# Preactivation convolution chain: the sums over the batch of layers 1 and 3 made by GpSimd instead of VectorE

## The chip, the cores and the metric

The kernel runs on 1 core of one Trainium2 chip. The metric is device time in microseconds (us), the median of several executions of the whole kernel. Times in the trace are us from the start of the span of one profiled execution.

## The reference, cut to what matters

```python
x = x + L0(gn(x))          # x is [32, 32, 32, 32], float32
x = x + L1(gn(x))
x = x + L2(gn(x))
x = x + L3(gn(x))

def L0(x, weight, bias_p, gamma, beta):         # L2 is the same with its own arrays
    wb = sign(weight) * mean(abs(weight))       # one 3x3 kernel for each place of the image
    out = einsum('bchwk,ochwk->bohw', patches(x), wb) + bias_p
    mean, var = out.mean((0, 2, 3)), out.var((0, 2, 3))      # one of each a channel
    out = relu(gamma * (out - mean) * rsqrt(var + 1e-5) + beta)
    return sign(out) * mean(abs(out))
```

L1 is a convolution with weights of its own for each place, without signs or statistics; L3 multiplies x, its squares and all products of pairs in a row by weights. `gn` is a normalisation over 16 groups of channels. In the kernel the layers are numbered 0 to 3; the change is in layers 0 and 2. The mean of `out` needs the sum of the convolution's result over the batch (32 samples) for each channel and place: 128 partitions x 256 places, kept in `row_sums`. The sum of its product with the bias, a part of the variance, is made from the same array.

## The kernel before

The image lies in SBUF as 128 partitions x 8 blocks (`BLOCKS`, index m) x 1024 elements, with the batch innermost. A convolution layer runs over 32 chunks (n = 4m + j); each has a weight load of 1152 KB, a stretch of matmuls called a piece here, and a stage on each of the other engines. The engines' programs are written out in order by hand, each with semaphores to the others. In layers 0 and 2, for chunk n:

- SyncE loads the weights into one of 8 slots of `wring`, once both VectorE and ScalarE are done with chunk n - 8.
- GpSimd (loop over n at the end of `xn_of`, `low_half`, `copy_near`): two operations of `xn_of` (L267) normalise piece e = n + 6 into a ring of 4; `low_half` (L372) waits for ScalarE's `high_half` and writes the low float16 half of piece n + 5; `copy_near` (L383) waits until piece n - 4 has been multiplied and copies the neighbours. The normalisation ends with e = 31, at n = 25; from n = 26 on only `copy_near` is left. The first 8 pieces are normalised by VectorE (`FRONT`).
- ScalarE: `high_half` (L517) of piece n + 6, which waits for `xn_of` of that piece; `load_beyond` (L526), two DMAs of 32 KB that bring rows of the neighbouring blocks, for which the pieces up to n + 4 must be normalised and piece n - 4 multiplied; `sign_of` (L509 and L510) on the weights; for n % 4 in (1, 2) and n > 4, `square_half` (L537) on a half of an earlier block's result.
- TensorE: piece n, once `near` and `beyond` of n are there and the signs of n are made. The two PSUM banks of a block must be free before its pieces 0 and 1.
- VectorE: the sum of the absolute weights of chunk n (L747), and after chunks 4m + 3 and 4m + 4 `evacuate(e)` for e = 2m and 2m + 1: it waits until the bank's pieces are done, transposes the bank from PSUM into `scratch` (L739), and reduces the 32 batch elements of each of 16 places into `row_sums` (L741).

After the last piece the chain goes over `evacuate(15)`, the sum of the absolute sums (L757), the bias product (L760) and some twenty small operations to the batch statistics of the layer, and from there to the next layer.

`sum_squares` on GpSimd (L393, L397) is not changed, but is built like the added code: in layers 0 and 1, before the convolution, it adds halves of 1024 elements in five steps with a wait for GpSimd's own semaphore after each of the first four:

```python
while width > B:
    pool.tensor_tensor(sq[:, 0:width], sq[:, 0:width], sq[:, width:2 * width], ALU.add).then_inc(halved, 1)
    halvings[0] += 1
    pool.wait_ge(halved, halvings[0])
    width //= 2
```

Of the kernel before, what the change touches and what calls it, by code (L numbers as in the profile page):

```python
# [9 lines left out]
ALU = mybir.AluOpType  # L10
ACT = mybir.ActivationFunctionType
X = mybir.AxisListType.X

P = 128
B = C = H = W = 32
# [5 lines left out]
BLOCKS = 8  # L21
PIECES = 4
# [52 lines left out]
def build(nc, x, w_conv, bias, gamma_beta, w_pairs, mats, sel_rows, sel_index, out):  # L75
    ctx = ExitStack()
    with ctx:
        def sb(name, shape, dt):
            return ctx.enter_context(nc.sbuf_tensor(name, shape, dt))

        def sem(name):
            return ctx.enter_context(nc.semaphore(name))

        def sems(name, n):
            return [sem(f"{name}{i}") for i in range(n)]
# [13 lines left out]
        stats = sb("stats", [P, 6, 512], F32)  # L99
# [6 lines left out]
        row_sums = sb("row_sums", [P, BLOCKS * W], F32)  # L106
# [43 lines left out]
        bank_free = sems("bank_free", 2)  # L150
# [20 lines left out]
        abs_red = sems("abs_red", 2)  # L171
        abs_total = sems("abs_total", 2)
        rows_summed = sem("rows_summed")
        rows_squared = sem("rows_squared")
        bn_sums_in = sems("bn_sums_in", 2)
        bn_sums = sems("bn_sums", 2)
# [34 lines left out]
        states = [(state_a, state_b), (state_a, state_b), (state_b, state_a)]  # L211

        def blk(t, m):
            return t[:, m * BLOCK:(m + 1) * BLOCK]

        def rows_of(t, e):
            return t[:, e * 512:(e + 1) * 512]

        def normed(layer, m, j):
            aux = states[layer][1]  # L220
            first = (m + 1) * BLOCK + j * PIECE
            return aux[:, first:first + PIECE]
# [5 lines left out]
        def order(m, j):  # L228
            return 2 * j + m if m < 2 else PIECES * m + j

        def needed(n):

            m, j = divmod(n, PIECES)
            return order(min(m + 1, BLOCKS - 1), j)
# [13 lines left out]
        def wait_normed(eng, layer, e):  # L248
            if layer == 1 and e < FRONT:
                eng.wait_ge(front_made, FRONT + e + 1)  # L250
            else:
                eng.wait_ge(norm_made[layer], e + 1 - (FRONT if layer == 1 else 0))
# [99 lines left out]
        def _(pool):  # L352
# [6 lines left out]
            def xn_of(layer, e, made):  # L359

                if layer != 1:
                    pool.wait_ge(norm_made[layer], e - XSLOTS + 1)
                sub, mul = normalise(pool, layer, e)
                sub().then_inc(centred, 1)
                centre[0] += 1
                pool.wait_ge(centred, centre[0])
                mul().then_inc(made, 1)

            def low_half(layer, e):
                pool.wait_ge(hi_made, CHUNKS * (layer // 2) + e + 1)  # L370
                hv = halves(layer, e)
                pool.tensor_tensor(hv[:, 1, :], xn_ring[:, e % XSLOTS, :], hv[:, 0, :], ALU.subtract).then_inc(norm_made[layer], 1)  # L372

            def copy_near(layer, n):

                m, j = divmod(n, PIECES)
                wait_normed(pool, layer, order(m, j))
                if n >= PIECES:
                    pool.wait_ge(conv_done, CHUNKS * layer + n - PIECES + 1)
                dst, src = near[:, j, :], normed(layer, m, j)  # L380
                if layer != 1:
                    dst, src = dst.bitcast(F16), src.bitcast(F16)
                pool.tensor_copy(dst, src).then_inc(near_made, 1)  # L383
# [3 lines left out]
            def sum_squares(layer, m):  # L387

                pool.wait_ge(squares[layer], m + 1)
                sq = blk(states[layer][1], m)  # L390
                width = BLOCK // 2
# [4 lines that stand above are left out]
                    width //= 2  # L396
                pool.tensor_tensor(red[:, 1, m * B:(m + 1) * B], sq[:, 0:B], sq[:, B:2 * B], ALU.add).then_inc(gn_red_pool[layer], 1)  # L397

            for layer in range(3):
                if layer < 2:  # L400
                    for m in range(DVE_SQUARES, BLOCKS):
                        sum_squares(layer, m)
                pool.wait_ge(gn_ready[layer], 1)
                ready = 0
                for n in range(CHUNKS):
                    upto = min(CHUNKS, needed(n) + 3)
                    for e in range(ready, upto):
                        if e >= FRONT:
                            xn_of(layer, e, norm_made[1] if layer == 1 else xn_made)
                        if layer != 1 and e:  # L410
                            low_half(layer, e - 1)
                        if layer != 1 and e == CHUNKS - 1:
                            low_half(layer, e)
                    ready = max(ready, upto)
                    copy_near(layer, n)

            def copy_ring(k):

                if k % (2 * GROUP) == 0 and k < NK:
                    pool.wait_ge(parts_in[k // GROUP // 2] if k else half_in, 16 * 2 * G)  # L420
                if k == GROUP:
                    pool.wait_ge(parts_in[0], 16 * 2 * G)
                if k >= GROUP:
                    pool.wait_ge(gathered, (k - GROUP + 1) * PT)
                for side in range(2):
                    if side:
                        pool.wait_ge(ring_made, 2 * k + 1)
                    pool.tensor_copy(ring[side * 2 * W:(side + 1) * 2 * W, k % GROUP, :].rearrange("p (g n) -> p g n", g=G),  # L428
                                     parts[0:2 * W, k // KPART % 2, :, k % KPART * C4 * B:(k % KPART + 1) * C4 * B]
                                     ).then_inc(ring_made, 1)  # L430
                pool.wait_ge(ring_made, 2 * k + 2)
# [213 lines left out]
        def _(dve):  # L645
# [26 lines left out]
            def sum_rows(side, src, m, layer):  # L672
                dve.tensor_reduce(red[:, side, m * B:(m + 1) * B], blk(src, m).rearrange("p (h b) -> p b h", b=B), X,
                                  ALU.add).then_inc(gn_red[layer], 1)

            for layer in range(3):
# [10 lines left out]
                width = MB if layer < 2 else 512  # L687
# [16 lines left out]
                if layer == 1:  # L704
# [4 lines left out]
                    for e in range(2 * BLOCKS):  # L709
                        m, h = divmod(e, 2)  # L710
# [17 lines left out]
                m2 = layer // 2  # L728
# [5 lines left out]
                def evacuate(e):  # L734

                    m, h = divmod(e, 2)
                    raw = rows_of(scratch, e).rearrange("p (w b) -> p w b", b=B)
                    dve.wait_ge(conv_done, CHUNKS * layer + PIECES * m + 3 + h)
                    dve.transpose(raw, psum[:, h, :].rearrange("p (w o) -> p w o", o=C)).then_inc(bank_free[h], 1)  # L739
                    dve.wait_ge(bank_free[h], 1 + BLOCKS * layer + m + 1)  # L740
                    dve.tensor_reduce(row_sums[:, e * 16:(e + 1) * 16], raw, X, ALU.add).then_inc(rows_summed, 1)  # L741

                for n in range(CHUNKS):
                    dve.wait_ge(w_in[slot(layer, n)], 16 * loads(layer, n))
                    if n == 0 and m2:
                        dve.wait_ge(abs_red[0], 1)
                    dve.tensor_reduce(abs_sums[:, n:n + 1], wring[:, slot(layer, n), 0:ABS_DVE],  # L747
                                      X, ALU.add, apply_absolute_value=True).then_inc(abs_made, 1)
                    if n % PIECES == 3:
                        evacuate(2 * (n // PIECES))  # L750
                    if n % PIECES == 0 and n:
                        evacuate(2 * (n // PIECES) - 1)
                evacuate(2 * BLOCKS - 1)

                dve.wait_ge(abs_made, CHUNKS * (m2 + 1))
# [357 lines left out]
```

## Time and profile before

| | us |
|---|---|
| median of 3 runs | 734.14 (733.12 to 734.63) |
| the profiled execution's own time | 732.94 |
| its span, first to last instruction | 731.1 |
| VectorE busy | 566.7 (78%) |
| TensorE busy | 497.6 (68%) |
| ScalarE busy | 431.5 (59%) |
| GpSimd busy | 420.1 (57%) |

The busy times are sums over a program with stages of different kinds, so the shares of the whole say little of one stage. The convolution of layer 0 takes the span from about 40 to 141 us, that of layer 2 from about 328 to 427 us; the rows below are taken inside these two. Engines are PE (TensorE), DVE (VectorE), ACT (ScalarE), POOL (GpSimd) and SP (SyncE); ACTq is ScalarE's sequencer, which issues its DMAs. L383 is line 383 of the kernel.

### The profile page before, as it was taken

What the parts mean: (1) busy time and instruction counts of PE and PEld (TensorE: products, weight loads), DVE (VectorE), ACT (ScalarE), POOL (GpSimd) and SP (SyncE); (2) the same over time, 40 slices, a digit from 0 to 9 for tenths busy, and PEclk for the clock granted to TensorE, in tenths of its full rate; (3) what the DMA queues carried; (4) which work ended last, traced back from release to release, by engine and by line L of the source; (5) the groups of instructions that cost most, each with busy time, mean ns of one, the idle gap of its engine ahead of it and who ended that gap; (6) DMA issues with size and microseconds to landing.
All of it is one profiled execution on the core that took longest, in us unless ns stands there. A gap on an engine that the chain in (4) does not pass through costs nothing.

```text
span 731.1 us, 53320 instructions
## 1 busy us (share of the span) xinstructions
PE 497.6 (68%) x24392; PEld 388.3 (53%) x24392; DVE 566.7 (78%) x709; ACT 431.5 (59%) x717; POOL 420.1 (57%) x653
## 2 busy tenths in 40 slices
PE   3546656609479999806666623626898888887898
PEld 4535655509368888605656521204565555554565
DVE  4799999898833635389999989955688788887787
ACT  5359999574011212317999938324567766666665
POOL 3388885004445651029888200537779878878672
PEclk9858889758799999955888975966899999999999
DMA  8949999500179999946999930015789999999996
GB/s 329 422 146 397 400 399 397 231 0 1 32 275 376 379 390 392 412 192 230 395 395 398 368 138 0 1 26 163 270 302 402 368 353 406 364 340 384 333 387 246
DMA packets 38882, 209.09 MB, mean 286 GB/s; under 512 B 7216, under 2 KB 14384, under 8 KB 18352
## 3 DMA queue, kind: packets, MB, share of 16 engines
q1 hardware_dynamic: 29376, 201.67, 72.2%
q10 hardware_dynamic: 9216, 6.30, 2.8%
q0 software_dynamic: 240, 0.53, 0.2%
q8 instruction: 22, 0.36, 0.2%
q14 instruction: 28, 0.23, 0.1%
HBM read 193.79 MB, written 4.19 MB: 271 GB/s over the span
## 4 chain that ended last, share of the span: by engine, by line
PE 37%; DVE 19%; DMA 13%; issue 11%; ACT 9%; POOL 8%; ACTq 2%; SPq 0%; DVEq 0%; POOLq 0%
PE psum L902 15%; PE psum L1015 7%; DMA wring<-in_pairs 6%; PE psum L989 5%; PE psum L926 5%; ACT signs L510 4%; DMA beyond<-state_b 4%; POOL xn_ring L267 3%; ACT state_b L640 2%; DVE state_b L862 2%; DVE state_a L807 2%; PE psum L1001 2%; DMA beyond<-state_a 2%; POOL state_a L372 2%; ACTq L526 2%
## 5 line engine op out<-in xcount | busy, mean ns | idle before, releaser
L862 DVE TENSOR_TENSOR state_b<-psum,state_b 128x512 f32<-128x512 f32 x256 | 167.6, 686 | 52.2 <-ACT state_b L640 48.2
L902 PE MATMUL psum<-signs,near 64*32 64x96 f16 (+3 forms) x6528 | 128.8, 221 | 98.1 <-DMA beyond<-nothing 37.8
L640 ACT ACTIVATE state_b<-psum 128x512 f32<-128x512 f32 x256 | 142.0, 595 | 81.3 <-PE psum L989 77.0
L902 PEld LDWEIGHTS psum<-signs,near 64*32 64x32 f16 (+1 forms) x6528 | 116.1, 105 | 106.8 <-issue 106.3
L747 DVE TENSOR_REDUCE abs_sums<-wring 128x1 f32<-128x2048 f32 x64 | 142.8, 2276 | 0.1
L510 ACT ACTIVATE signs<-wring 128x2304 f16<-128x2304 f32 x64 | 134.9, 2108 | 0.0
L1015 PE MATMUL psum<-state_b,wring 128*32 128x32 f32 x8192 | 104.5, 201 | 11.0 <-issue 5.3
L1015 PEld LDWEIGHTS psum<-state_b,wring 128*32 128x32 f32 x8192 | 86.9, 112 | 40.6 <-issue 21.6
L902 PE MATMUL psum<-wring,near 64*32 64x96 f32 (+5 forms) x3264 | 96.2, 242 | 14.8 <-DMA beyond<-nothing 10.5
L989 PE MATMUL psum<-signs,sel 64*128 64x512 f16 x516 | 88.1, 395 | 26.2 <-POOL signs L428 13.9
L428 POOL COPY signs<-wring 64x512 f16<-64x512 f16 x130 | 85.7, 659 | 30.7 <-PE psum L989 24.3
L902 PEld LDWEIGHTS psum<-wring,near 64*32 64x32 f32 (+1 forms) x3264 | 87.7, 109 | 21.8 <-issue 19.8
L383 POOL COPY near<-state_b 128x512 f16<-128x512 f16 (+1 forms) x64 | 34.4, 539 | 66.7 <-PE psum L902 33.8
L902 PE MATMUL psum<-signs,beyond 32*32 32x96 f16 (+2 forms) x2176 | 65.6, 218 | 0.0
L902 PEld LDWEIGHTS psum<-signs,beyond 32*32 32x32 f16 x2176 | 56.4, 103 | 4.8
L447 POOL COPY wring<-state_b 32x256 f32<-32x256 f32 x128 | 50.6, 395 | 10.1
L713 DVE STREAM_TRANSPOSE state_b<-psum 128x512 f32<-128x512 f32 x16 | 11.5, 717 | 57.6 <-PE psum L912 57.0
L989 PEld LDWEIGHTS psum<-signs,sel 64*128 64x128 f16 x516 | 23.8, 93 | 47.5 <-ACT state_b L640 25.5
L902 PE MATMUL psum<-wring,beyond 32*32 32x96 f32 (+2 forms) x1088 | 48.8, 239 | 0.0
L571 ACT ACTIVATE signs<-state_a 128x1024 f32<-128x1024 f32 x8 | 8.5, 1058 | 67.3 <-PE psum L912 60.5
L393 POOL TENSOR_TENSOR state_b<-state_b 128x512 f32<-128x512 f32 (+3 forms) x24 | 16.7, 698 | 54.0 <-ACT state_b L501 52.6
L372 POOL TENSOR_TENSOR state_a<-xn_ring,state_a 128x256 f16<-128x256 f32 x32 | 22.3, 698 | 41.2 <-ACT state_a L517 41.1
(153 smaller groups left out, 881.6 us busy)
## 6 DMA issues: line engine op xcount, KB each, us to landing
wring<-in_w SPq DMA_DIRECT2D x96, 1152.0 KB, 10.2
wring<-in_pairs SPq DMA_DIRECT2D x64, 1152.0 KB, 9.0
state_a<-in_x SPq DMA_DIRECT2D x8, 512.0 KB, 9.9
beyond<-state_b ACTq DMA_DIRECT2D x112, 32.0 KB, 5.9
wring<-signs SPq DMA_DIRECT2D x56, 64.0 KB, 4.9
out<-state_a SPq DMA_DIRECT2D x7, 512.0 KB, 10.8
beyond<-state_a ACTq DMA_DIRECT2D x56, 32.0 KB, 6.1
beyond<-nothing ACTq DMA_DIRECT2D x24, 32.0 KB, 4.7
```

The costliest lines, as they stand in the source:

```text
L372: pool.tensor_tensor(hv[:, 1, :], xn_ring[:, e % XSLOTS, :], hv[:, 0, :], ALU.subtract).then_inc(norm_made[layer], 1)
L383: pool.tensor_copy(dst, src).then_inc(near_made, 1)
L428: pool.tensor_copy(ring[side * 2 * W:(side + 1) * 2 * W, k % GROUP, :].rearrange("p (g n) -> p g n", g=G), parts[0:2 * W, k // KPART % 2, ...
L447: pool.tensor_copy(own_x[beside * W:(beside + 1) * W, g % 2, cols], x_sq[g * W:(g + 1) * W, half, :]).then_inc(own_copied, 1)
L510: act.activation(signs[:, n % PIECES, :], wring[:, slot(layer, n), :], ACT.Sign).then_inc(signs_made, 1)
L640: act.activation(left[:, n % LSLOTS, :], psum[:, n % ASLOTS, :], ACT.Copy, scale=1.0 / HALF_SCALE / HALF_SCALE).then_inc(left_made, 1)
L747: dve.tensor_reduce(abs_sums[:, n:n + 1], wring[:, slot(layer, n), 0:ABS_DVE], X, ALU.add, apply_absolute_value=True).then_inc(abs_made, 1)
L862: dve.tensor_tensor(feats[:, n % FSLOTS, :], psum[:, ASLOTS + n % BSLOTS, :], left[:, n % LSLOTS, :], ALU.mult).then_inc(feats_made, 1)
L902: last = pe.matmul(psum[g * B:(g + 1) * B, bank, (a * C) % 512:(a * C) % 512 + (b - a) * C], acts[q, j, s, k, :], weights[q, j, kind, s, ( ...
L926: pe.matmul(psum[:, 4, first * B:end * B], same_half, by_h[:, h, first:end, :], start=(first == 0 and h == 0), stop=(h == H - 1), skip_gro ...
L989: last = pe.matmul(psum[:, bank, :], sel[half, t % PT * P:(t % PT + 1) * P], ring[half, t // PT, :], start=True, stop=True)
L1015: last = pe.matmul(psum[g * W:(g + 1) * W, 6 + s // HALF, col:col + B], wt[:, t % PT, c, g, :], f[:, g, c, :], start=False, stop=(t % (HAL ...
```

## The change

In layers 0 and 2 `evacuate` on VectorE keeps only the transpose. GpSimd gets `sum_rows(layer, e)`: it waits for the transpose of half block e, adds the upper half of the batch to the lower in five steps (16 places x 16, 8, 4, 2, 1 results a partition), with a wait for its own semaphore after every step, and writes the same 16 columns of `row_sums`. Sixteen calls a layer: after `copy_near` of n = 5, 7, 9, ..., 31 (e = 0 to 13), and e = 14 and 15 behind the loop. VectorE waits for `rows_summed` before the bias product, as it did.

```diff
@@ -396,6 +397,27 @@
+            added = [0]
+
+            def sum_rows(layer, e):
+
+                m2 = layer // 2
+                pool.wait_ge(bank_free[e % 2], 1 + BLOCKS * layer + e // 2 + 1)
+                raw = rows_of(states[layer][1], e).rearrange("p (w b) -> p w b", b=B)
+                tree = stats[:, 1, :].rearrange("p (k w b) -> p k w b", k=2, b=B // 2)
+                width = B // 2
+                src = raw
+                while width > 1:
+                    dst = tree[:, width.bit_length() % 2, :, 0:width]
+                    pool.tensor_tensor(dst, src[:, :, 0:width], src[:, :, width:2 * width], ALU.add).then_inc(rows_added, 1)
+                    added[0] += 1
+                    pool.wait_ge(rows_added, added[0])
+                    src = dst
+                    width //= 2
+                pool.tensor_tensor(row_sums[:, e * 16:(e + 1) * 16].unsqueeze(2), src[:, :, 0:1], src[:, :, 1:2], ALU.add
+                                   ).then_inc(rows_summed, 1)
+                pool.wait_ge(rows_summed, 2 * BLOCKS * m2 + e + 1)
+
@@ -413,6 +435,10 @@
                             low_half(layer, e)
                     ready = max(ready, upto)
                     copy_near(layer, n)
+                    if layer != 1 and n > PIECES and n % PIECES in (1, 3):
+                        sum_rows(layer, 2 * (n // PIECES - 1) + n % PIECES // 2)
+                for e in range(2 * BLOCKS - 2, 2 * BLOCKS) if layer != 1 else ():
+                    sum_rows(layer, e)
@@ -737,8 +763,6 @@
                     dve.transpose(raw, psum[:, h, :].rearrange("p (w o) -> p w o", o=C)).then_inc(bank_free[h], 1)
-                    dve.wait_ge(bank_free[h], 1 + BLOCKS * layer + m + 1)
-                    dve.tensor_reduce(row_sums[:, e * 16:(e + 1) * 16], raw, X, ALU.add).then_inc(rows_summed, 1)
```

## Rows read from the trace of the kernel before

**Rows 1.** Busy time by window, two stretches of each changed layer.

```profile
core 0: us, PE busy (x) PEld busy (x) DVE busy (x) ACT busy (x) POOL busy (x), PEclk, DMA share, GB/s
55.53:113.04 57.51, 37.52 (x2604) 34.17 (x2608) 55.79 (x40) 57.51 (x97) 50.20 (x77) 0.83 1.02 398
342.10:399.17 57.07, 39.31 (x2581) 35.44 (x2585) 54.64 (x39) 56.80 (x97) 50.14 (x77) 0.80 1.02 395
113.04:140.74 27.70, 18.59 (x1354) 16.78 (x1336) 25.42 (x20) 25.03 (x37) 7.49 (x13) 0.88 0.94 366
399.17:427.39 28.22, 17.68 (x1360) 15.91 (x1360) 26.47 (x21) 25.03 (x37) 7.51 (x13) 0.94 0.96 370
```

**Rows 2.** Timeline: `copy_near` of n = 5 and 24, and ScalarE's signs of n = 24.

```profile
55.53 0.61 POOL L383 COPY near<-state_b 128x512 f16<-128x512 f16 x1
113.04 0.61 POOL L383 COPY near<-state_b 128x512 f16<-128x512 f16 x1
...
115.37 2.11 ACT L510 ACTIVATE signs<-wring 128x2304 f16<-128x2304 f32 x1
...
342.10 0.61 POOL L383 COPY near<-state_a 128x512 f16<-128x512 f16 x1
399.17 0.61 POOL L383 COPY near<-state_a 128x512 f16<-128x512 f16 x1
```

**Rows 3.** Waits of GpSimd, 55 to 113 us and then 342 to 399 us.

```profile
POOL state_b L372 <- ACT state_b L517: 5.8, 10, 0.6
...
POOL state_a L372 <- ACT state_a L517: 5.4, 9, 0.6
```

**Rows 4.** Groups of instructions, 60 to 100 us: busy, mean ns, idle before.

```profile
L747 DVE TENSOR_REDUCE abs_sums<-wring 128x1 f32<-128x2048 f32 x14 | 31.3, 2276 | 0.0
...
L267 POOL TENSOR_TENSOR xn_ring<-xn_ring,stats 128x256 f32<-128x256 f32 x14 | 10.2, 730 | 1.1
...
L372 POOL TENSOR_TENSOR state_b<-xn_ring,state_b 128x256 f16<-128x256 f32 x13 | 8.7, 672 | 4.0 <-ACT state_b L517 4.0
L383 POOL COPY near<-state_b 128x512 f16<-128x512 f16 x13 | 7.9, 611 | 0.0
...
L739 DVE STREAM_TRANSPOSE state_b<-psum 128x512 f32<-128x512 f32 x7 | 5.0, 707 | 1.4 <-PE psum L902 1.4
...
L741 DVE TENSOR_REDUCE row_sums<-state_b 128x16 f32<-128x512 f32 x7 | 4.8, 686 | 0.2
```

**Rows 5.** Groups of instructions on GpSimd, whole span: halvings of `sum_squares`.

```profile
L393 POOL TENSOR_TENSOR state_b<-state_b 128x512 f32<-128x512 f32 x6 | 7.7, 1281 | 52.6 <-ACT state_b L501 52.6
L393 POOL TENSOR_TENSOR state_b<-state_b 128x256 f32<-128x256 f32 x6 | 4.4, 733 | 0.5
L393 POOL TENSOR_TENSOR state_b<-state_b 128x128 f32<-128x128 f32 x6 | 2.7, 457 | 0.5
L393 POOL TENSOR_TENSOR state_b<-state_b 128x64 f32<-128x64 f32 x6 | 1.9, 321 | 0.5
L397 POOL TENSOR_TENSOR stats<-state_b 128x32 f32<-128x32 f32 x6 | 1.5, 253 | 0.5
```

**Rows 6.** Timeline of ScalarE's sequencer, the two issues of one `load_beyond`.

```profile
111.92 0.51 ACTq L526 DMA_DIRECT2D beyond<-state_b  x1
...
112.46 0.61 ACTq L526 DMA_DIRECT2D beyond<-state_b  x1
```

**Rows 7.** The chain that ended last, end of layer 0's convolution: start, length.

```profile
132.73 6.26 DMA beyond<-state_b
...
139.08 1.64 PE psum L902 x128
...
140.74 0.73 DVE state_b L739
...
142.09 0.21 DVE abs_sum L757
142.30 0.34 DVE stats L760
```

More of the change, by code:

```diff
@@ L173, in build @@
         rows_summed = sem("rows_summed")
+        rows_added = sem("rows_added")
         rows_squared = sem("rows_squared")
```

## Prediction

> **What bounds the kernel now.** I read the page first, then busy time by window, because the shares of the whole mix stages. Inside the two changed layers I cut two stretches: A, from GpSimd's copy_near of n = 5 to that of n = 24 (19 stages), and B, from there to the end of the convolution. [Rows 1] show that in A nothing is idle but TensorE: ScalarE is busy 57.51 us of 57.51 in layer 0 and 56.80 of 57.07 in layer 2, VectorE 55.79 and 54.64, GpSimd 50.20 and 50.14, the DMA share is 1.02. So the question is how much room GpSimd has, and whether relief of VectorE is worth anything.
>
> Next I read the waits of GpSimd alone. In A it waits 5.8 us in layer 0 and 5.4 us in layer 2, all of it in front of low_half for ScalarE's high_half [rows 3]. Without these waits its 19 stages take 57.51 - 5.8 = 51.7 us and 57.07 - 5.4 = 51.7 us, so 2.72 us a stage. That agrees with the groups: 2 x 0.730 + 0.672 + 0.611 = 2.74 us of operations [rows 4]. One block (4 stages) is 10.9 us of GpSimd against a pace of 57.51 / 19 x 4 = 12.1 us. **The room is 1.2 us a block, 0.6 us for each of the two added sums.** In B there is much: 7.5 us of work in 28 us [rows 1].
>
> GpSimd and ScalarE go in lockstep in A. ScalarE can't take high_half of a piece before GpSimd's xn_of of it, and everything behind high_half in ScalarE's program (load_beyond, the signs) waits with it. TensorE needs the beyond and the signs. So a late GpSimd stage is a late stage of everything.
>
> **The price of one sum.** The trace has no sum_rows, but the halvings of sum_squares are the same instruction at the sizes 256, 128, 64 and 32: 733, 457, 321, 253 ns [rows 5]. The size 16 isn't there; the last two steps differ by 68 ns for 32 elements, so 253 - 34 = 219 ns. Sum 1.98 us. Each wait for GpSimd's own semaphore leaves 0.5 / 6 = 0.08 us idle [rows 5], and sum_rows has five: 0.40 us. As instructions there overlap their neighbours' ends by some hundredths, I take **2.35 us**. Lower bound: 1.98 us, with no gap at all. Upper bound: the operands are 16 short rows with a stride, and no row shows such rows; if every element cost as two do, the steps cost as 512, 256, 128, 64 and 32: 1.281 + 0.733 + 0.457 + 0.321 + 0.253 = 3.05, with the gaps 3.45 us. I take the low side because the xn_of operations, with a mean broadcast over 8 rows, cost 730 ns [rows 4], as the plain 256 does.
>
> The Trainium skill (GPSIMD Engine Reference, section 7, Performance pitfalls) says that reads from SBUF whose inner step is above 8 bytes cost some 2.9 cycles an element in place of 1.9. No row of this trace shows such a read. Only the last step, with 16 results, has an inner step of 64 bytes; at the 1.2 GHz with which section 3.1 of that page reckons, an estimate by it is 16 more cycles, 0.01 us a sum. Were all 496 results of the five steps to pay it, the estimate would be 0.4 us a sum, which would make the change about 9 us dearer than I forecast.
>
> **Stretch A.** Ten sums fall in it (n = 5, 7, ..., 23). If GpSimd now sets the pace, its waits for ScalarE go, since ScalarE needs 12.1 us a block and GpSimd 10.9 + 2 x 2.35 = 15.6. The stretch takes 51.7 + 23.5 = 75.2 us. Layer 0: 75.2 - 57.5 = +17.7. Layer 2: 75.2 - 57.1 = +18.1. **Together +35.8 us.**
>
> Does the added wait for the transpose cost more? Behind it in GpSimd's queue is the next xn_of, for which all wait. For even e it needs piece n - 3 multiplied. That piece's beyond is issued about 1.6 us into its GpSimd stage, is there some 0.5 + 6.3 us after that, the matmuls take 1.6 us or somewhat more [rows 6, 7], the transpose 0.7 [rows 4]: about 11 us after the start of stage n - 3. Stage n gets to its sum at 3 x 2.72 + 2.35 + 2.72 = 13.2 us. VectorE sits free in front of the transpose by then. I take 0, with a margin of 2 us; at slower matmuls, 0.5 us for each even e would be 5 us in all.
>
> **What VectorE gains: 0.** It loses 16 reductions of 0.686 us a layer [rows 4], 11 us, and goes from 4 x 2.276 + 2 x (0.707 + 0.686) = 11.9 us a block to 10.5. Nothing takes it up in A, where it then waits for GpSimd's pace; in B ScalarE is the next limit. If the sums cost GpSimd nothing, ScalarE's 12.1 us a block would still cover it.
>
> **Stretch B.** GpSimd has per block 4 x 0.61 + 2 x 2.35 = 7.1 us of work in some 11 to 12 us, and its copy_near runs ahead of TensorE, so the sums are hidden there. ScalarE is the limit again at its old pace, but starts B less behind GpSimd: now its signs of n = 24 begin 115.37 - 113.04 = 2.33 us after GpSimd's copy [rows 2]. When it has waited for GpSimd, only the two issues of load_beyond, 0.51 + 0.61 us [rows 6], and 0.4 us for the absolute values lie between high_half and the signs, which comes to 1.0 us after the copy. **-1.3 us a layer, -2.6.** The last piece in layer 0 waits for a beyond that takes 6.26 us under a full DMA load until 139.0 [rows 7], where ScalarE's last signs end near 137.6. In the changed kernel the weights have been loaded ahead, and the beyond lands earlier, so up to this 1.4 us come back: **-1.3**. In layer 2 the next weights are being loaded at that time either way: 0.
>
> **The end of each convolution.** Now from the end of the transpose, 140.74 + 0.73 = 141.47, to the bias product at 142.30 it is 0.83 us, with the reduction and L757 in it [rows 7]. In the changed kernel GpSimd must finish e = 15: 2.35 us and two hand-overs of some hundredths, 2.40 us, with L757 beside it. e = 14 is done by then, as its transpose comes a piece earlier. 2.40 - 0.83 = 1.57 us a layer, **+3.1 us**.
>
> **Sum.** 35.8 - 2.6 - 1.3 + 3.1 = **+35.0 us**. The profiled execution took 732.94 us (span 731.1), so 767.9; the median of the runs is 1.2 us above it, so **769 us**.
>
> **Rivals.**
> - *The short rows are dear* (chance 0.09). Price 3.45 us: 20 x 1.1 = +22 in A and +2.2 at the ends, so +59 us, 793 us. For it: no row has operands of this form. Against it: the broadcast rows of xn_of cost nothing.
> - *More is given back in B* (0.08). ScalarE is busy only 25.03 us of 27.70 and 28.22 [rows 1]. If all of its idle there went, 2.7 + 3.2 us, in place of the 1.3 that I took for the last beyond, the result is 4.6 us lower, 764 us; with the price at its lower bound (20 x 0.37 + 0.7 = 8 us less), 756 us.
> - *GpSimd's load stays hidden* (0.03). If the lockstep had more play than I read, only the ends remain: +3 us, 737 us. Against it: the waits of [rows 3] are all the slack there is.
> - *VectorE is the bound, and its relief counts* (0.03). SyncE's loads wait for VectorE's sums of absolute weights as well as for the signs, and VectorE is busy 97% of A [rows 1]. If it sets the pace through the weight slots, 16 reductions a layer come off: 2 x 11.0 = -22, and +3 at the ends, 715 us. It decides where a sum costs GpSimd less than its 0.6 us of room. Five instructions at 0.18 us, what the halvings extrapolate to at no element at all (253 - 32 x 2.1), are already 0.9 us.
>
> **The numbers.** My forecast has a chance of 0.77. The range takes in the lower price with more given back (756) and most of the way to the dear price (793): 755 to 788, with something above for dear rows and something below for the two rivals near or under the old time. Faster by over 0.2% (about what a measurement of this kernel can tell) is the last rival, 0.03; within 0.2% is 0.01; slower is the rest, 0.96.
>
> **What the profile should show.** (1) Five steps of sum_rows near 733, 457, 321, 253 and 219 ns, a sum in 2.3 to 2.4 us. (2) In A GpSimd at about 98% of a stretch of 75 us with no waits for ScalarE; ScalarE and VectorE with gaps, the DMA share down to about 0.8. (3) The chain that ended last running through GpSimd's L267, L372, L383 and the new line in both layers. (4) Some 2.4 us between the last transpose and the bias product. (5) Layer 1 and layer 3 as they were. **What would make it wrong:** steps whose time doesn't follow the count of elements; waits for the transposes in front of the first step; a play between GpSimd and ScalarE that takes several us.

## The result and the profile after

The changed kernel takes 770.56 us (median of 4 runs, 765.71 to 776.52) against 733.75 us. The ratio of the executions is 1.0488, with a 95% interval of 1.0441 to 1.0535, so the kernel is slower by 32 to 39 us; the medians differ by 36.8 us. Ratios here leave out executions more than 1.5% above the fastest of their kernel, and are not exactly the quotients of the medians. Forecast were 769 us, between 755 and 788. The profiled execution took 772.41 us, with a span of 770.6.

The title counts the layers from 1; here, as in the kernel, the changed ones are layers 0 and 2. Stretch A runs from GpSimd's copy_near of n = 5 to that of n = 24, and stretch B from there to the start of the last transpose. First the groups of instructions on GpSimd over the whole span. These are the five steps of sum_rows, the first once from each of the two state tensors; the halvings to compare them with are in [rows 5]:

```profile
L412 POOL TENSOR_TENSOR stats<-stats 128x128 f32<-128x128 f32 x32 | 14.5, 452 | 2.5
...
L412 POOL TENSOR_TENSOR stats<-state_a 128x256 f32<-128x256 f32 x16 | 11.7, 730 | 8.3 <-DVE state_a L765 8.2
L412 POOL TENSOR_TENSOR stats<-state_b 128x256 f32<-128x256 f32 x16 | 11.7, 730 | 6.8 <-DVE state_b L765 6.7
L412 POOL TENSOR_TENSOR stats<-stats 128x64 f32<-128x64 f32 x32 | 10.2, 318 | 2.5
...
L412 POOL TENSOR_TENSOR stats<-stats 128x32 f32<-128x32 f32 x32 | 7.6, 239 | 2.5
L417 POOL TENSOR_TENSOR row_sums<-stats 128x16 f32<-128x16 f32 x32 | 6.9, 214 | 2.5
```

730 + 452 + 318 + 239 + 214 ns = 1.95 us. The first four are as the halvings of the same size or a little below, so the 16 short rows cost nothing that can be seen. The last step, whose operands lie 64 bytes apart, has no halving of its size: it is 5 ns below what the halvings give for 16 results (219), and 9 ns above what its own neighbour gives (239 - 16 x 2.1 = 205). The idle column shows 2.5 / 32 = 0.08 us before each step.

Now a piece of the chain that ended last, inside stretch A of layer 0 (start, length). The chain is nothing but GpSimd's own work:

```profile
101.56 0.55 POOL near L384
102.11 0.70 POOL stats L412
102.81 0.07 issue
...
104.12 0.23 POOL row_sums L417
104.34 0.07 issue
104.41 0.73 POOL xn_ring L268
```

The 0.07 us of issue behind each step is the wait for the engine's own semaphore. The next xn_of starts only after the fifth of them. The chain gives a sum 104.41 - 102.11 = 2.30 us, but it cuts instructions where they overlap. The timeline of the same place shows the copies that begin and end the stages:

```profile
98.83 0.61 POOL L384 COPY near<-state_b 128x512 f16<-128x512 f16 x1
...
101.50 0.61 POOL L384 COPY near<-state_b 128x512 f16<-128x512 f16 x1
...
106.52 0.61 POOL L384 COPY near<-state_b 128x512 f16<-128x512 f16 x1
```

A stage without a sum takes 101.50 - 98.83 = 2.67 us, one with a sum 5.02. **A sum lengthens its stage by 2.35 us.** Nine stages of the one kind and ten of the other make 9 x 2.67 + 10 x 5.02 = 74.2 us.

The same stretches as in [rows 1], A of both layers and then B of both layers:

```profile
core 0: us, PE busy (x) PEld busy (x) DVE busy (x) ACT busy (x) POOL busy (x), PEclk, DMA share, GB/s
55.15:129.60 74.45, 48.28 (x2781) 43.69 (x2771) 50.82 (x31) 61.05 (x98) 68.90 (x128) 0.71 0.95 355
358.04:432.28 74.24, 47.27 (x2728) 43.04 (x2732) 50.20 (x30) 61.20 (x98) 68.83 (x128) 0.71 0.94 358
129.60:155.21 25.61, 15.40 (x1171) 13.82 (x1156) 20.12 (x13) 23.12 (x35) 16.82 (x37) 0.87 0.68 253
432.28:459.70 27.42, 18.87 (x1216) 17.22 (x1216) 20.84 (x13) 23.23 (x35) 16.31 (x36) 0.74 0.63 235
```

Stretch A grew by 74.45 - 57.51 = 16.9 us and 74.24 - 57.07 = 17.2 us. ScalarE, at 100% before, is idle for 13 us of it now; VectorE, at 97%, for 24 us. GpSimd is busy for 68.9 us (93%), and the other 5.5 us are gaps between its instructions; no wait for another engine is listed in either stretch. Stretch B shrank by 27.70 - 25.61 = 2.1 us in layer 0 and by 28.22 - 27.42 = 0.8 us in layer 2.

The transfers fell less than the stretch grew: 355 GB/s x 74.45 us are 26.4 MB in A of layer 0, where it was 398 x 57.51 = 22.9 MB, and B has 6.5 MB in place of 10.1. So some three of the weight loads of 1152 KB moved from B into A.

Last the end of layer 0, on GpSimd and then on VectorE:

```profile
153.16 0.73 POOL L412 TENSOR_TENSOR stats<-state_b 128x256 f32<-128x256 f32 x1 [4.32 <-DVE state_b L765]
...
156.07 0.73 POOL L412 TENSOR_TENSOR stats<-state_b 128x256 f32<-128x256 f32 x1 [0.64 <-DVE state_b L765]
156.88 1.17 POOL L412 TENSOR_TENSOR stats<-stats 128x128 f32<-128x128 f32 x3
158.13 0.21 POOL L417 TENSOR_TENSOR row_sums<-stats 128x16 f32<-128x16 f32 x1
...
155.21 0.72 DVE L765 STREAM_TRANSPOSE state_b<-psum 128x512 f32<-128x512 f32 x1 [2.20 <-PE psum L926]
155.85 0.18 DVE L781 TENSOR_REDUCE abs_sum<-abs_sums 128x1 f32<-128x64 f32 x1
158.38 0.42 DVE L784 TENSOR_TENSOR stats<-row_sums,bias 128x256 f32<-128x256 f32 x1 [2.35 <-POOL row_sums L417]
```

VectorE has its transpose done at 155.93 and starts the bias product at 158.38, 2.45 us later. In the same view of the kernel before it is 142.22 - 141.46 = 0.76 us (0.83 in [rows 7], where the chain again cuts the overlap). From the start of the last transpose it is 3.17 us in place of 1.48.

Up to the bias product of layer 2, which starts at 462.95 us instead of 428.87, 34.1 of the 39.5 us between the two profiled spans have arisen. The other 5.4 us arose in layer 3, which isn't changed; the last experiments are on them.

### The profile page after: what moved, and what is told of

It reads as the page before. It is cut to its first block, busy times and chain, and to the rows that moved or that the text cites. A ratio compares the mean times of both kernels' runs of the same rounds, so it can differ in the third digit from the quotient of the medians.

```text
span 770.6 us, 53474 instructions
## 1 busy us (share of the span) xinstructions
PE 518.3 (67%) x24392; PEld 405.4 (53%) x24392; DVE 544.5 (71%) x677; ACT 436.5 (57%) x717; POOL 480.2 (62%) x813
## 4 chain that ended last, share of the span: by engine, by line
PE 34%; POOL 24%; DVE 17%; issue 8%; DMA 7%; ACT 6%; SPq 2%; ACTq 1%; POOLq 0%; DVEq 0%
PE psum L926 14%; POOL xn_ring L268 7%; PE psum L1039 5%; POOL stats L412 5%; PE psum L1013 5%; PE psum L950 4%; DMA wring<-in_pairs 4%; POOL near L384 3%; POOL signs L454 2%; ACT signs L536 2%; DVE xn_ring L268 2%; DVE state_a L831 2%; POOL state_a L373 2%; DMA beyond<-state_b 2%; PE psum L1025 2%
## 5 line engine op out<-in xcount | busy, mean ns | idle before, releaser
L926 PE MATMUL psum<-signs,near 64*32 64x96 f16 (+3 forms) x6528 | 145.1, 236 | 113.0 <-DMA beyond<-nothing 35.7
L926 PEld LDWEIGHTS psum<-signs,near 64*32 64x32 f16 (+1 forms) x6528 | 130.9, 114 | 122.4 <-issue 120.0
L926 PE MATMUL psum<-signs,beyond 32*32 32x96 f16 (+2 forms) x2176 | 73.5, 231 | 0.0
L384 POOL COPY near<-state_b 128x512 f16<-128x512 f16 (+1 forms) x64 | 34.1, 536 | 58.3 <-PE psum L926 26.8
L926 PEld LDWEIGHTS psum<-signs,beyond 32*32 32x32 f16 x2176 | 63.3, 111 | 5.7
L473 POOL COPY wring<-state_b 32x256 f32<-32x256 f32 x128 | 50.4, 394 | 10.1
L1013 PEld LDWEIGHTS psum<-signs,sel 64*128 64x128 f16 x516 | 23.8, 93 | 46.5 <-ACT state_b L666 24.7
L926 PEld LDWEIGHTS psum<-wring,beyond 32*32 32x32 f32 x1088 | 43.2, 106 | 3.5 <-issue 0.3
L950 PE MATMUL psum<-state_a,mats_sb 128*128 128x96 f32 (+1 forms) x256 | 33.9, 303 | 16.2 <-DMA state_a<-in_x 11.0
```

Of the source, the lines that this page charges most:

```text
L473: pool.tensor_copy(own_x[beside * W:(beside + 1) * W, g % 2, cols], x_sq[g * W:(g + 1) * W, half, :]).then_inc(own_copied, 1)
L926: last = pe.matmul(psum[g * B:(g + 1) * B, bank, (a * C) % 512:(a * C) % 512 + (b - a) * C], acts[q, j, s, k, :], weights[q, j, kind, s, ( ...
L950: pe.matmul(psum[:, 4, first * B:end * B], same_half, by_h[:, h, first:end, :], start=(first == 0 and h == 0), stop=(h == H - 1), skip_gro ...
L1013: last = pe.matmul(psum[:, bank, :], sel[half, t % PT * P:(t % PT + 1) * P], ring[half, t // PT, :], start=True, stop=True)
```

## The experiments

Each ratio is against the kernel before, run beside it on the same chip. The kernel before had medians of 732.5 to 736.8 us there, and single executions of 724.8 to 741.1, so it scatters more than its first runs had shown; the 95% intervals are given for that reason. In the diffs, three dots stand for what is left out.

**VectorE's relief alone** (no_sums). The sums over the batch are left out on VectorE, and GpSimd does nothing in their place; `row_sums` is set to zero at the start.

```diff
                     dve.transpose(raw, psum[:, h, :].rearrange("p (w o) -> p w o", o=C)).then_inc(bank_free[h], 1)
-                    dve.wait_ge(bank_free[h], 1 + BLOCKS * layer + m + 1)
-                    dve.tensor_reduce(row_sums[:, e * 16:(e + 1) * 16], raw, X, ALU.add).then_inc(rows_summed, 1)
...
-                dve.wait_ge(rows_summed, 2 * BLOCKS * (m2 + 1))
+                dve.wait_ge(bank_free[1], 1 + BLOCKS * (layer + 1))
```

> The kernel before without its reductions on VectorE and with nothing in their place: the sums over the batch in both layers are left out (row_sums stays at zero). My theory (VectorE's relief is worth nothing beside ScalarE at 100% and the weight DMA at its full share): only the 0.6 us behind the last transpose of each layer goes, 733.7 - 1.2 = 732.5 us, 731.5 to 733.5. Rival (VectorE sets the pace through the weight slots): 16 x 0.686 us a layer come off, 712 us.

Measured: 729.46 us against 732.51, ratio 0.9973 (0.9933 to 1.0013). That is 2 us less by the ratio and 3 by the medians, with an interval that includes no change. The median lies 2 us below the expected range, and the kernel before ran 1.2 us below the 733.7 on which that range was built. The windows of stretch A in both layers:

```profile
54.76:111.51 56.75, 35.36 (x2596) 32.22 (x2600) 50.11 (x30) 56.75 (x97) 50.12 (x78) 0.89 1.02 397
343.49:400.18 56.69, 35.59 (x2580) 32.30 (x2581) 49.09 (x30) 56.69 (x97) 50.06 (x77) 0.88 1.02 395
```

VectorE falls from 55.8 to 50.1 us of busy time in A of layer 0, and ScalarE stays at 100%. The rival of 712 us is refuted. The stretches are 0.8 and 0.4 us shorter than in the first profile of the kernel before, but that is no gain of the relief: with VectorE's reductions in place the same stretch took 57.51, 57.07, 56.70 and 58.13 us in the two profiles of the kernel before, and 56.70 to 56.72 us in the unchanged layers of the kernels layer0_only, layer2_only and delay48 below. What the relief does give is at the two ends, where the bias product starts 0.75 us after the last transpose in place of 1.48: 1.5 us in all.

**GpSimd's load alone** (both_sum). VectorE reduces as before; GpSimd does all of sum_rows as well.

```diff
                     dve.transpose(raw, psum[:, h, :].rearrange("p (w o) -> p w o", o=C)).then_inc(bank_free[h], 1)
+                    dve.wait_ge(bank_free[h], 1 + BLOCKS * layer + m + 1)
+                    dve.tensor_reduce(row_sums[:, e * 16:(e + 1) * 16], raw, X, ALU.add).then_inc(rows_summed, 1)
...
-                pool.tensor_tensor(row_sums[:, e * 16:(e + 1) * 16].unsqueeze(2), src[:, :, 0:1], src[:, :, 1:2], ALU.add
-                                   ).then_inc(rows_summed, 1)
-                pool.wait_ge(rows_summed, 2 * BLOCKS * m2 + e + 1)
+                pool.tensor_tensor(tree[:, 1, :, 0:1], src[:, :, 0:1], src[:, :, 1:2], ALU.add).then_inc(rows_added, 1)
+                added[0] += 1
+                pool.wait_ge(rows_added, added[0])
...
                 dve.wait_ge(rows_summed, 2 * BLOCKS * (m2 + 1))
+                dve.wait_ge(rows_added, 10 * BLOCKS * (m2 + 1))
```

> VectorE reduces as in the kernel before, and GpSimd does the whole of sum_rows as well, with its last step into a spare column. My theory (all of the loss is GpSimd's load): the stretch of 19 stages at 74.4 us as in the changed kernel, the end of each layer as there, so 765 to 772 us, as the changed kernel. Rival (the loss has a part that comes from VectorE's changed timing, such as late transposes): below 760 us. Rival (VectorE's relief has given something back in the changed kernel): above 774 us.

Measured: 769.55 us, ratio 1.0511 (1.0420 to 1.0602). Stretch A takes 74.97 and 75.08 us. The whole loss is there with VectorE's work unchanged. A is 0.5 and 0.8 us longer than in the changed kernel; GpSimd waits 0.6 and 0.8 us for a transpose in it.

**The same sums where GpSimd has room** (late_four). Only e = 10 to 13 go to GpSimd, and count on a semaphore of their own, for which VectorE waits before the bias product.

```diff
+                if e not in (10, 11, 12, 13):
+                    return
                 m2 = layer // 2
                 pool.wait_ge(bank_free[e % 2], 1 + BLOCKS * layer + e // 2 + 1)
...
+                    if e in (10, 11, 12, 13):
+                        return
+                    dve.wait_ge(bank_free[h], 1 + BLOCKS * layer + m + 1)
+                    dve.tensor_reduce(row_sums[:, e * 16:(e + 1) * 16], raw, X, ALU.add).then_inc(rows_summed, 1)
```

> Only the sums e = 10 to 13 of each layer, which fall after GpSimd's last xn_of, are moved to GpSimd; the other twelve stay reductions on VectorE. My theory (there GpSimd has 20 us of room for 9.4 us of sums): 733.7 us, 732.5 to 735. Rival (any sum on GpSimd costs its 2.35 us, wherever it stands): 8 x 2.35 = +19, 752 us. If VectorE's relief of 2.7 us a layer counted in this part: 728 us.

Measured: 734.26 us against 732.51, ratio 1.0043 (1.0008 to 1.0079). The windows of stretch B in the two layers:

```profile
112.35:140.16 27.81, 17.46 (x1360) 15.64 (x1351) 22.87 (x15) 25.03 (x37) 15.14 (x33) 0.94 0.93 361
400.48:428.90 28.42, 18.05 (x1365) 16.24 (x1360) 22.77 (x16) 25.02 (x37) 15.16 (x33) 0.93 0.95 369
```

GpSimd's busy time there doubles from 7.5 to 15.1 us, and the stretches stay at 27.8 and 28.4 us (27.7 and 28.2). So a sum costs 2.35 us in stretch A and nothing that can be seen in B: the eight sums would be 19 us at the full price. The interval of the ratio reaches from 0.6 to 5.8 us above the kernel before. The profile shows 1.5 us before layer 3 (the bias product of layer 2 starts at 430.4 us), and 0.4 us of these in the four stretches; the rest lies in parts of the program that the edit doesn't touch.

**A small dose and a middle one** (two_steps, three_steps). Only the last two or the last three steps of the tree are left. The diff is that of two_steps; three_steps has `width = 4`.

```diff
-                width = B // 2
+                width = 2
                 src = raw
```

> The changed kernel with only the last two of the five steps (32 and 16 results a partition) in each sum_rows; the three large steps are left out, so it sums 4 of the 32 samples. A sum then takes 0.24 + 0.21 + 2 x 0.08 = 0.61 us. My theory (room of 0.6 us for each sum between GpSimd and ScalarE): the room is just used up, 733 to 739 us. Rival (lockstep without play: each sum adds its whole time in both layers): 20 x 0.61 = +12, 746 us.

> The changed kernel with the last three steps (64, 32 and 16 results) in each sum_rows; the two large ones are left out, so it sums 8 of the 32 samples. A sum takes 0.32 + 0.24 + 0.21 + 3 x 0.08 = 1.01 us. GpSimd then needs 10.7 + 2.0 = 12.7 us a block against ScalarE's 12.1: +0.6 us a block, 4.75 blocks in two layers, +6 us, and the ends are about as before: 738 to 743 us. Rival (each sum adds its whole time): +20, 754 us. Rival (the play is larger than read): 734 us.

Measured: 735.88 us, ratio 1.0068 (1.0031 to 1.0104), and 742.33 us, ratio 1.0079 (1.0038 to 1.0119). By the ratios the two are some 5 and 6 us dearer than the kernel before, with intervals of about 2 to 9 us, far from the 12 and 20 us of a lockstep without play. Both medians lie in the expected ranges. The ratios don't tell the two doses apart; the profiles do. Stretch A of the two_steps kernel, then of the three_steps kernel:

```profile
54.21:113.02 58.81, 37.27 (x2561) 33.94 (x2565) 49.75 (x30) 57.90 (x97) 54.17 (x98) 0.82 1.02 396
339.97:400.95 60.98, 38.63 (x2576) 34.98 (x2576) 49.44 (x30) 59.03 (x97) 54.17 (x98) 0.81 1.02 395
```

```profile
53.95:116.47 62.52, 42.10 (x2576) 38.32 (x2576) 50.18 (x30) 59.29 (x97) 57.22 (x107) 0.74 1.02 395
342.48:406.34 63.86, 41.22 (x2576) 37.13 (x2576) 50.12 (x30) 58.86 (x97) 57.33 (x107) 0.79 1.01 393
```

GpSimd's own time would give 50.9 + 10 x 0.61 = 57.0 us and 50.9 + 10 x 1.01 = 61.0 us (50.9 is 74.4 less ten sums of 2.35). Measured are 58.8 and 61.0, 62.5 and 63.9. What lies above is a wait for the transposes: the profile lists 1.5 and 3.5 us of it in A of two_steps, and 1.5 and 2.7 us in three_steps. GpSimd's timeline in the three_steps kernel:

```profile
66.68 0.61 POOL L384 COPY near<-state_b 128x512 f16<-128x512 f16 x1
68.75 0.32 POOL L412 TENSOR_TENSOR stats<-state_b 128x64 f32<-128x64 f32 x1 [1.47 <-DVE state_b L765]
```

In the changed kernel, whose stages are longer, the transposes have more time: its first profile lists no such wait in A of either layer, its second 0.4 us in layer 0. It is a second price of the change, which shows mainly when the first one is small.

**The dose doubled** (twice). The five steps stand in a loop of two rounds; in the first round the last one goes to a spare column of `tree`.

```diff
+                for again in range(2):
...
+                    if again == 0:
+                        pool.tensor_tensor(tree[:, 1, :, 0:1], src[:, :, 0:1], src[:, :, 1:2], ALU.add).then_inc(rows_added, 1)
```

> The changed kernel with every sum made twice by GpSimd (4.7 us a sum). My theory: 10 more sums of 2.35 us in each of the two long stretches, +47 us, and at each end e = 14 and e = 15 stand behind each other, +2.35 to +4.7 us: 820 to 828 us. GpSimd has 2.4 + 9.4 = 11.8 us of work for a block after its last xn_of too, so a few us more may come there. Rival (part of the loss is not GpSimd's time, but a fixed effect of the moved work): below 805 us.

Measured: 829.98 us, ratio 1.1237 (1.1187 to 1.1287). The rival below 805 us is refuted, and the time is 2 us above the expected range. Stretch A takes 98.06 and 97.99 us, 23.6 and 23.8 more than in the changed kernel for ten more sums, so 2.36 to 2.38 us each. From the copy of n = 24 to the bias product layer 0 takes 36.5 us (28.8 in the changed kernel): behind the last transpose e = 14 and 15 are still queued up behind e = 13, and the bias product starts 11.1 us after that transpose in layer 0 and 9.2 us in layer 2, where it is 3.2 in the changed kernel.

**The two last sums of each layer back on VectorE** (ends_back). GpSimd's sums have a semaphore of their own here too.

```diff
+                if e not in tuple(range(14)):
+                    return
...
+                    if e in tuple(range(14)):
+                        return
+                    dve.wait_ge(bank_free[h], 1 + BLOCKS * layer + m + 1)
+                    dve.tensor_reduce(row_sums[:, e * 16:(e + 1) * 16], raw, X, ALU.add).then_inc(rows_summed, 1)
```

> The changed kernel with e = 14 and 15 of each layer back on VectorE. My theory: only the 1.6 us at the end of each layer come back, 770 - 3.2 = 767 us (764 to 770). Rival (GpSimd's e = 14 was late as well and held up e = 15): more than 5 us come back.

Measured: 765.68 us, ratio 1.0358 (1.0306 to 1.0410). In its profile the bias product of layer 2 starts at 459.13 us, 3.8 us before that of the changed kernel (462.95) and 4.5 us before that of its second profile (463.60). The two ends give 3.5 us of this against the first profile (3.17 + 3.25 - 2 x 1.48) and 4.1 us against the second (3.85 + 3.17 - 2 x 1.48); the rest is scatter of other parts. That the ends can give more than the 3.2 us expected is seen in the second profile of the changed kernel. Its GpSimd at the end of layer 0:

```profile
154.65 0.73 POOL L412 TENSOR_TENSOR stats<-state_b 128x256 f32<-128x256 f32 x1 [4.30 <-DVE state_b L765]
...
157.00 0.73 POOL L412 TENSOR_TENSOR stats<-state_b 128x256 f32<-128x256 f32 x1
...
159.06 0.21 POOL L417 TENSOR_TENSOR row_sums<-stats 128x16 f32<-128x16 f32 x1
```

The last two transposes start at 153.80 and 155.46 us there, 1.66 us apart, which is less than a sum. So e = 15 waits for e = 14, and the bias product starts 3.85 us after the start of the last transpose, against 3.17 in the first profile and 1.48 in the kernel before. The rival was right here in part, with 0.7 us of the layer, but not with its more than 5 us. The same is seen in layer 0 of both_sum and layer0_only (1.35 and 1.52 us apart, 4.24 and 4.00 us), and not in layer 2 of both profiles of the changed kernel, of both_sum and of layer2_only, where the last two transposes were 2.3 to 3.0 us apart.

**One layer at a time** (layer0_only, layer2_only).

```diff
-                    if layer != 1 and n > PIECES and n % PIECES in (1, 3):
+                    if layer == 0 and n > PIECES and n % PIECES in (1, 3):
```

This is layer0_only; layer2_only has `layer == 2`. In the other layer VectorE reduces as before, and the two calls behind the loop follow the same condition.

> The change in layer 0 alone; layer 2 keeps its reductions on VectorE. My theory, from the profile of the changed kernel: +16.9 in the long stretch, -2.1 behind it, +1.6 at the end, so +16 us over the kernel before. If a further effect of the changed layers on layer 3 exists, it should not show here, since layer 2 lies between: the time from layer 2's bias product to the end stays near 302 us.

> The change in layer 2 alone. My theory: +17.2, -0.8, +1.6, so +18 us over the kernel before, and together with layer 0 alone the +34 us of the changed kernel's two layers. If layer 3 takes longer because of what layer 2 did before it, this run is at +23 us and its time from the bias product to the end is some 5 us above 302.

Measured: 752.18 us, ratio 1.0272 (1.0195 to 1.0350), and 750.08 us, ratio 1.0260 (1.0184 to 1.0335). The bias product of layer 2 starts 18.0 and 17.8 us after that of the kernel before. By the ratios alone each layer costs 13 to 26 us; the profiles show that each carries half of the loss. Neither shows an effect on the other: A of the unchanged layer takes 56.71 us in both kernels.

**Where the other 5 us of the first profile come from** (delay48, after_again, before_again). The first is the kernel before, with chained operations at the end of layer 2's convolution:

```diff
                 dve.wait_ge(rows_summed, 2 * BLOCKS * (m2 + 1))
+                for _ in range(48 if m2 else 0):
+                    link(dve.tensor_tensor(tmp_a[:, 0:512], mean[:, 0:512], mean[:, 0:512], ALU.mult))
```

> The kernel before with 48 chained operations of VectorE (128x512, 0.70 us and 0.02 us each) put in at the end of layer 2's convolution: about 34 us in which TensorE idles, and no other change. It tells what layer 3 does if it only starts later. In the profile of the changed kernel the bias product of layer 2 was 34.0 us later and the end 39.5 us later. If the further 5.5 us come from where layer 3's start falls against TensorE's clock, this kernel's layer 3 (from the last delay to the end) may differ from the 302 us of before by several us, and its runs differ among themselves. If they come from the changed layers themselves, layer 3 takes 302 us as before.

> The changed kernel, profiled a second time. Bias product of layer 2 at 462 to 464 us of the span as in the first profile. If the 307.7 us from there to the end were chance of that execution, they come out anywhere from 300 to 308; if they belong to the change, 306 to 309 again.

> The kernel before, profiled a second time, to see how far its own layer 3 scatters: 302 us from the bias product of layer 2 to the end in the first profile. The theory of chance says several us of scatter here too; the other theory says 302 again.

Measured: delay48 766.99 us, ratio 1.0404 (1.0354 to 1.0454), so 29.8 us (26 to 33) for a delay that was 34.9 us long in its profile. Its profiled span is 33.7 us longer than that of the kernel before. Layer 3 took 305.7 us there, 3.5 more, and the last transpose of layer 2 started at 422.72 us, 4.7 us earlier than in the kernel before, though the two programs are the same up to that point. The second profile of the changed kernel has a time of 766.70 us, that of the kernel before 729.07. Busy time from layer 2's bias product to the end, of the first and the second profile of the changed kernel and of the second profile of the kernel before:

```profile
462.95:770.60 307.65, 227.36 (x10802) 144.20 (x10802) 235.55 (x366) 180.38 (x329) 200.64 (x309) 0.89 0.71 258
463.60:764.90 301.30, 225.51 (x10802) 143.27 (x10802) 236.53 (x366) 180.29 (x329) 200.13 (x309) 0.91 0.72 264
429.07:727.30 298.23, 225.97 (x10804) 143.74 (x10804) 235.95 (x367) 180.35 (x330) 199.90 (x309) 0.90 0.72 266
```

The changed kernel has 307.7 and 301.3 us, the kernel before 302.2 and 298.2, the others between 302.4 (no_sums) and 306.8 (twice). So layer 3, with the same instructions, scatters by several us from execution to execution in both kernels, and the 5.4 us are not shown to belong to the change. With two profiles a kernel the mean of layer 3 is 304.5 against 300.2. Over all profiles, those with sums on GpSimd in stretch A of layer 2 have 301.3 to 307.7 us and those without 298.2 to 305.7, too few and too close to say that there is no effect at all. This stays open.

Layer 3 isn't the only part that scatters. From the bias product of layer 0 to the first copy of layer 2 it is 184.0 and 183.9 us in the two profiles of the kernel before, but 181.1 in delay48, 186.0 in late_four and 187.6 in no_sums, none of which changes anything in between. These profiles come from more than one chip, so part of the scatter may lie between chips. So no difference of 2 or 3 us between two spans is a finding here; the stretches of the changed layers are what can be compared.

## Why the prediction was right, step by step

- **The price of a sum**: forecast 2.35 us, measured 2.35 (5.02 - 2.67), with steps of 730, 452, 318, 239 and 214 ns for 733, 457, 321, 253 and 219. The dear rows of the first rival (3.45 us) did not appear. By the Trainium skill (GPSIMD Engine Reference, section 7) the last step, with its reads 64 bytes apart, would pay a surcharge of 0.01 us, which is an estimate from the page's figures. This case can neither show nor exclude it: the 214 ns are 5 ns below one extrapolation and 9 ns above the other.
- **The room of 0.6 us for each sum**: right. At a price of 0.61 us GpSimd's own time came to the old length of the stretch (57.0 us), and the growth of 1.3 and 3.9 us was the wait for the transposes; at 2.35 us the stretch grew by 17, at twice that by 41. The sentence that in A nothing is idle but TensorE is too wide, though: GpSimd was busy 50.20 of 57.51 us, and the room was found in what was left.
- **Stretch A**: forecast +17.7 and +18.1, measured +16.9 and +17.2. The price was right; the stage without a sum is 2.67 us instead of 2.72, which over 19 stages is the 0.8 to 0.9 us.
- **GpSimd at 98% and a DMA share of 0.8 in A**: wrong, at no cost to the sum. GpSimd was busy 93%, since the forecast's own 51.7 us had counted the gaps between instructions as work. The DMA share was 0.95, since loads of B moved into A.
- **VectorE's gain 0**: right for A, where no_sums shows nothing beyond the scatter of the unchanged stretch. Its 1.5 us are the reductions at the two ends, which the forecast has in the 0.83 us of its sum for the ends.
- **The wait for the transposes, taken as 0**: right in the changed kernel (0 to 0.4 us in a stretch). It isn't nothing at smaller prices: 1.5 to 3.5 us a layer.
- **Stretch B**: forecast -2.6 and -1.3, measured -2.1 and -0.8, and the rows part it as the forecast did. These are ScalarE's signs of n = 24 and of n = 31 in the changed kernel, in layer 0 and in layer 2:

```profile
130.80 2.11 ACT L536 ACTIVATE signs<-wring 128x2304 f16<-128x2304 f32 x1
...
151.19 2.11 ACT L536 ACTIVATE signs<-wring 128x2304 f16<-128x2304 f32 x1
...
433.75 2.11 ACT L536 ACTIVATE signs<-wring 128x2304 f16<-128x2304 f32 x1
...
453.91 2.11 ACT L536 ACTIVATE signs<-wring 128x2304 f16<-128x2304 f32 x1
```

  The signs of n = 24 begin 1.20 and 1.47 us after GpSimd's copy, where the forecast had 1.0 and the kernel before 2.33 and 2.34: -1.1 and -0.9 us for -1.3 each. The last transpose starts 1.91 us after the end of the last signs in layer 0, where it was 3.21: -1.3, as forecast, and the two transfers of the last beyond landed in 1.8 and 1.9 us there, where the chain of before had one of 6.26 [rows 7]. In layer 2 it is 3.68 us after 3.73: 0, as forecast.
- **The ends**: forecast +1.57 each, measured +1.69 and +1.77 in the first profile, and +2.37 and +1.69 in the second. The sentence "e = 14 is done by then" was the weak one: the last two transposes can be 1.66 us apart, and a sum takes 2.35.
- **The sum**: forecast +35.0, of which the profiles show +34.1 up to the bias product of layer 2, and +34.5 in the second (463.60 - 429.07). It is so close because the misses partly cancel: -1.7 us in A, +1.0 in B, +0.3 at the ends, and -0.6 of scatter in the parts between. That the median is within 2 us of the forecast is luck in part: the medians moved by 36.8 us, and the unchanged layers alone scatter by more than the difference.

## What to carry to other kernels

Ask of the engine that takes over the work how much it may be late in the stretch where the work lands, not how busy it is over the whole: GpSimd was 57% busy, and had 0.6 us to spare for a sum of 2.35. In this kernel the waits of an engine in a lockstep were its room, and a dose of a few steps of the new work showed on the chip that it was used up. Relief of VectorE at 97% was worth nothing in A beside ScalarE at 100%. Work behind the last transpose of a layer should stay where it takes the least time: there VectorE's reduction of 0.69 us beat GpSimd's 2.35. And before a difference of a few us is explained, look how far the same stretch scatters in other profiles of unchanged code.

## What the runs showed of the hardware

TensorE's granted clock in stretch A was 0.83 and 0.80 of 2.4 GHz before and 0.71 in both layers of the changed kernel, where TensorE was idle for 26.2 of 74.45 us against 20.0 of 57.51 (layer 0). This cost next to nothing, as GpSimd set the pace: in the second profile of the changed kernel the clock was 0.68 and 0.73, and A took 74.75 and 74.26 us, with 0.4 us of waiting for a transpose in the first of them.

At the end of layer 2 one window of the changed kernel, 449.9 to 457.4 us, was granted 0.55, so nearly all of it at the lower level, 1.2 GHz. It is tempting to lay the long interval between the transposes of e = 13 and 14 at the clock's door. The same interval in both profiles of the changed kernel, then in both of the kernel before:

```profile
447.41:457.43 10.02, 6.72 (x416) 6.13 (x416) 7.26 (x6) 8.57 (x13) 3.29 (x8) 0.66 1.02 402
448.42:458.03 9.61, 6.13 (x410) 5.58 (x396) 7.26 (x6) 8.29 (x13) 3.29 (x8) 0.82 1.02 408
```

```profile
416.46:424.39 7.93, 6.26 (x416) 5.66 (x416) 7.89 (x7) 7.20 (x11) 0.36 (x1) 0.79 1.01 398
416.93:425.64 8.71, 5.78 (x397) 5.10 (x383) 7.97 (x7) 6.71 (x11) 0.00 (x0) 0.82 1.01 402
```

At 0.82 the changed kernel still needs 9.61 us, so the clock isn't the main cause. In both of its profiles TensorE stands idle for 3.2 to 3.4 us in this interval without a releaser that the profile names; for what it waits stays open. The last transpose isn't later for it: it follows the last signs by 3.68 us, as before.

The pairing of GpSimd and VectorE showed no cost for the operations seen here. GpSimd's step of 256 results took 730 ns in sum_rows, with VectorE busy 68% of stretch A, and 734 ns in sum_squares of the same kernel; VectorE's sum of absolute weights took 2260 ns each from 60 to 129 us, and 2275 ns from 60 to 112 us in the kernel before.
